# Last three steps of a two-convolution kernel written out on alternating PSUM banks, with a new way to finish and store the last half

## What is computed

```python
def reference(x, L0_conv_weight, L0_conv_threshold, L1_conv_kernel, L1_conv_bias):
    # x: (16, 32, 128, 128) float32
    # _gn: mean and variance over 16 groups of 2 channels, per image
    x = x + _L0_conv_ref(_gn(x), L0_conv_weight, L0_conv_threshold)   # 3x3, padding 1, weights masked by a score
    x = x + _L1_conv_ref(_gn(x), L1_conv_kernel, L1_conv_bias)        # 5x5 by FFT, same size, plus a bias per channel
    return x
```

## Time and profile before

| what | value |
|---|---|
| median of 3 runs | 835.81 us (834.25 to 837.2) |
| the profiled execution's own time | 834.83 us |
| its span, first to last instruction | 833.0 us |
| TensorE busy | 757.8 us (91%) |
| VectorE, ScalarE, GpSimd busy | 605.1, 336.1, 266.7 us |
| TensorE's granted clock, mean | 0.980 |
| DMA, mean over the span | 181 GB/s |

### The profile page before, as it was taken

The page is one execution under the profiler, slowest core; times in us unless marked ns, Lnnn a source line. Parts: engine busy times, 40 slices in busy tenths (PEclk is TensorE's granted clock), DMA queues, the critical chain, the costliest instruction groups (busy, mean ns, idle before and its releaser), DMA issues.

```text
span 833.0 us, 67770 instructions
## 1 busy us (share of the span) xinstructions
PE 757.8 (91%) x32302; PEld 541.3 (65%) x32302; DVE 605.1 (73%) x949; ACT 336.1 (40%) x289; POOL 266.7 (32%) x165
## 2 busy tenths in 40 slices
PE   0585579999999999999999999999999999998795
PEld 0342247787767677777778667867778777766463
DVE  6598368787878879787878788897978785745241
ACT  0352225444443536354444435363634444443410
POOL 1042022233333333232333333332323333333221
PEclk9998879999999999999999999999999999999998
DMA  8979986899897979898998979798987576753124
GB/s 178 209 154 224 218 183 152 192 219 213 194 218 164 221 190 223 195 222 194 219 209 201 213 171 231 177 223 192 221 195 177 138 177 153 155 132 90 43 50 101
DMA packets 234118, 150.59 MB, mean 181 GB/s; under 512 B 18592, under 2 KB 227552, under 8 KB 229984
## 3 DMA queue, kind: packets, MB, share of 16 engines
q1 hardware_dynamic: 228768, 144.67, 78.9%
q10 hardware_dynamic: 4608, 4.23, 2.1%
q0 software_dynamic: 704, 1.25, 0.7%
HBM read 75.60 MB, written 33.59 MB: 131 GB/s over the span
## 4 chain that ended last, share of the span: by engine, by line
PE 87%; issue 4%; DMA 3%; SPq 2%; ACT 1%; DVE 1%; ACTq 0%; POOLq 0%; DVEq 0%; POOL 0%
PE psum L772 66%; PE psum L790 21%; DMA x_bands<-x_dram 1%; DMA mid_bands<-mid 1%; SPq L259 1%; SPq L251 1%; ACT mid_bands L394 0%; DVE bn_in L559 0%; ACTq L455 0%; ACT conv_out L424 0%; ACT x_hi L387 0%; POOLq L57 0%; ACT x_hi L379 0%; SPq L240 0%; SPq L275 0%
## 5 line engine op out<-in xcount | busy, mean ns | idle before, releaser
L360 POOL TENSOR_TENSOR mid<-mid,conv_out 128x512 f32<-128x512 f32 x122 | 246.7, 2052 | 512.3 <-ACT conv_out L424 512.3
L772 PE MATMUL psum<-x_hi,s_hi 32*64 32x512 f16 x6656 | 200.9, 383 | 16.7 <-ACTq L455 6.6
L772 PE MATMUL psum<-x_hi,s_lo 32*64 32x512 f16 x6656 | 198.6, 378 | 1.6 <-issue 1.6
L772 PE MATMUL psum<-x_lo,s_hi 32*64 32x512 f16 x6656 | 198.3, 380 | 0.9 <-issue 0.5
L772 PEld LDWEIGHTS psum<-x_hi,s_hi 32*64 32x64 f16 x6656 | 126.6, 105 | 79.8 <-issue 12.1
L772 PEld LDWEIGHTS psum<-x_hi,s_lo 32*64 32x64 f16 x6656 | 141.7, 104 | 45.8 <-issue 4.6
L772 PEld LDWEIGHTS psum<-x_lo,s_hi 32*64 32x64 f16 x6656 | 105.7, 104 | 79.6 <-issue 10.6
L650 DVE SCALAR_TENSOR_TENSOR mid<-psum,unscale,x_own 128x1024 f32<-128x1024 f32 x64 | 79.2, 1279 | 97.1 <-PE psum L790 96.6
L424 ACT ACTIVATE conv_out<-psum,bias,unscale 128x512 f32<-128x512 f32 x122 | 85.2, 778 | 83.4 <-PE psum L772 83.4
L379 ACT ACTIVATE x_hi<-x_bands 128x2304 f16<-128x2304 f32 x32 | 67.8, 2119 | 119.8 <-PE psum L790 116.9
L387 ACT ACTIVATE x_hi<-mid_bands 128x2560 f16<-128x2560 f32 x32 | 74.8, 2339 | 69.9 <-PE psum L790 67.9
(11 more groups left out here) (77 smaller groups left out, 335.6 us busy)
## 6 DMA issues: line engine op xcount, KB each, us to landing
x_own<-x_dram SPq DMA_DIRECT2D x128, 256.0 KB, 5.0
mid_bands<-mid SPq DMA_DIRECT2D x372, 80.0 KB, 2.7
out_dram<-mid SPq DMA_DIRECT2D x116, 256.0 KB, 5.0
x_bands<-x_dram SPq DMA_DIRECT2D x96, 288.0 KB, 6.1
x_bands<-x_dram SPq DMA_DIRECT2D x32, 272.0 KB, 6.1
mid_bands<-mid SPq DMA_DIRECT2D x124, 64.0 KB, 2.7
every_mv<-mv_scratch ACTq DMA_DIRECT2D x16, 256.0 KB, 4.1
out_dram<-mid SPq DMA_DIRECT2D x24, 128.0 KB, 2.4
```

What stands on the lines that cost most here:

```text
L360: nc.gpsimd.tensor_tensor(m, m, conv_out[:, b, :], ALU.add).then_inc(out_added, 1)
L772: ins = nc.tensor.matmul(psum[2 * C * J:2 * C * (J + 1), bank + i, :].rearrange("p (a w) -> p a w", a=A), w[quad(i), at:at + 2, :].rearran ...
```

## The change

Four things are changed. TensorE's three last steps are written out one after another instead of looping; they use banks 0 to 3, 4 to 7, and 0 to 3 in turn (bank5), after one wait for bank3_go. ScalarE raises x5_hi_go for them before it takes the preceding half out of PSUM, and for the last two waits for VectorE's take of the half two before. GpSimd adds the bias to the last half's mid early, after its adds for half 29 (the mid of half 31 is complete then and has been moved on). The last half is finished by VectorE alone, in two operations that each read two banks of PSUM, scale them and add mid; each group of two banks is stored by two transfers from SP and two from ScalarE's queue.

```diff
+        LAST = HALVES - 1
+        LAST_GROUPS = (slice(HALF_BANKS, BANKS), slice(0, HALF_BANKS))
+        def bank5(k):
+            return X3_BANK if k >= LATE and (k - LATE) % 2 == 0 else X5_BANK
...
# SP, in place of the two store_out calls for the last half
+                    elif k == LAST:
+                        for g, banks in enumerate(LAST_GROUPS):
+                            sp.wait_ge(last_out, g + 1)
+                            store_out(k, banks, range(Q // 2))
...
# GpSimd
-            for k in range(HALVES):
+            for k in range(LAST):
                 for b in range(BANKS if k < LATE else HALF_BANKS):
                     add_out(k, b)
+                if k == LATE:
+                    pool.wait_ge(norm2, HALVES)
+                    m = mid[:, LAST % MID_SLOTS, :, :]
+                    nc.gpsimd.tensor_scalar(m, m, bias[:, 0:1], None, ALU.add).then_inc(bias_added, 1)
...
# ScalarE
-                nc.scalar.activation(conv_out[:, b, :], psum[:, X5_BANK + b, :], ACT.Identity,
+                nc.scalar.activation(conv_out[:, b, :], psum[:, bank5(k) + b, :], ACT.Identity,
...
-                if has5(s - 1):
+                if s > HALVES + 1:
+                    act.wait_ge(late_out, s - HALVES - 1)
+                if has5(s) and s >= HALVES:
+                    act.drain().then_inc(x5_hi_go, 1)
+                if has5(s - 1) and s <= LAST + LAG:
                     k = s - 1 - LAG
                     for b in range(BANKS if k < LATE else HALF_BANKS):
                         take_conv5(k, b)
-                if s > HALVES:
-                    act.wait_ge(late_out, s - HALVES)
-                if has5(s):
+                if has5(s) and s < HALVES:
                     act.drain().then_inc(x5_hi_go, 1)
...
+            for g, banks in enumerate(LAST_GROUPS):
+                act.wait_ge(last_out, g + 1)
+                for j in range(Q // 2, Q):
+                    act.dma_start(own_rows(out[LAST // 2], LAST % 2, j)[:, A * banks.start:A * banks.stop, :],
+                                  as_rows(mid, j, LAST % MID_SLOTS, banks)).then_inc(out_stored[LAST % MID_SLOTS], 16)
...
# VectorE (take_late also reads bank5(k) instead of X5_BANK)
-            take_late(HALVES - 1)
-            add_late(HALVES - 1)
+            dve.wait_ge(b5_whole, LAST + 1)
+            dve.wait_ge(bias_added, 1)
+            for at in LAST_GROUPS:
+                m = mid[:, LAST % MID_SLOTS, at, :]
+                nc.vector.scalar_tensor_tensor(m, psum[:, bank5(LAST) + at.start:bank5(LAST) + at.stop, :], unscale[:, 1:2], m,
+                                               ALU.mult, ALU.add).then_inc(last_out, 1)
...
# TensorE (pairs5_high, singles5 and pairs5_low take the bank; whole_step's reg_add stands before pairs5_low as before)
-                pe.br_lt(step, HALVES, on_true="whole_step", on_false="before_last").branch_hint(hint)
-            with nc.body("before_last", valid_engines=only):
-                pe.br("last_steps")
-            with nc.body("last_steps", valid_engines=only):
-                pairs5_high()
-                singles5()
-                pairs5_low(step)
-                pe.br_lt(step, STEPS, on_true="last_steps", on_false="all_done")
-            nc.switch_bb("all_done")
+                pe.br_lt(step, HALVES, on_true="whole_step", on_false="last_steps").branch_hint(hint)
+            nc.switch_bb("last_steps")
+            pe.wait_ge(bank3_go, 1)
+            for k in range(LATE, HALVES):
+                pairs5_high(bank5(k))
+                singles5(bank5(k))
+                pairs5_low(bank5(k))
```

More of the change, by code:

```diff
@@ L172, in two_blocks @@
         late_added = sem("late_added")
+        bias_added = sem("bias_added")
+        last_out = sem("last_out")
         def has3(s):
@@ L241, in load_own, with store_out @@
                                  ).then_inc(x_own_in[h % X_SLOTS], 16)
-            def store_out(k, banks):
-                for j in range(Q):
+            def store_out(k, banks, quads=range(Q)):
+                for j in quads:
                     sp.dma_start(own_rows(out[k // 2], k % 2, j)[:, A * banks.start:A * banks.stop, :],
@@ L667, in take_late @@
                 at = slice(HALF_BANKS, BANKS)
-                nc.vector.tensor_scalar(conv_out[:, at, :], psum[:, X5_BANK + at.start:X5_BANK + at.stop, :],
+                nc.vector.tensor_scalar(conv_out[:, at, :], psum[:, bank5(k) + at.start:bank5(k) + at.stop, :],
                                         unscale[:, 1:2], bias[:, 0:1], ALU.mult, ALU.add).then_inc(late_out, 1)
@@ L812, in singles3, with pairs5_high, singles5, pairs5_low @@
                 singles(s3_hi, x3_lo, K3, X3_BANK).then_inc(c3_whole, 1)
-            def pairs5_high():
+            def pairs5_high(bank=X5_BANK):
                 pe.wait_ge(x5_hi_go, 1)
-                pairs(s5_hi, x5_hi, K5, X5_BANK, start=True, every=x5_hi_go)
-                pairs(s5_lo, x5_hi, K5, X5_BANK)
-            def singles5():
+                pairs(s5_hi, x5_hi, K5, bank, start=True, every=x5_hi_go)
+                pairs(s5_lo, x5_hi, K5, bank)
+            def singles5(bank=X5_BANK):
                 pe.wait_ge(x5_lo_go, 1)
[L823 to L830, removed]
+                singles(s5_hi, x5_lo, K5, bank)
+                singles(s5_hi, x5_hi, K5, bank)
+                singles(s5_lo, x5_hi, K5, bank).then_inc(a5_whole, 1)
+            def pairs5_low(bank=X5_BANK):
+                pairs(s5_hi, x5_lo, K5, bank, every=x5_lo_go).then_inc(b5_whole, 1)
             def mix_mean(stat):
@@ L897, in _ @@
                 singles5()
-                pairs5_low(step)
-                pe.br_lt(step, HALVES, on_true="whole_step", on_false="before_last").branch_hint(hint)
-            with nc.body("before_last", valid_engines=only):
-                pe.br("last_steps")
-            with nc.body("last_steps", valid_engines=only):
-                pairs5_high()
-                singles5()
-                pairs5_low(step)
-                pe.br_lt(step, STEPS, on_true="last_steps", on_false="all_done")
-            nc.switch_bb("all_done")
+                pe.reg_add(step, step, 1)
+                pairs5_low()
+                pe.br_lt(step, HALVES, on_true="whole_step", on_false="last_steps").branch_hint(hint)
[5 more added lines that the diff above has]
+                pairs5_low(bank5(k))
 _INS = ["x", "L0_conv_weight", "L0_conv_threshold", "L1_conv_kernel", "L1_conv_bias"]
```

## The result

Twenty runs of each kernel gave 838.18 us for the changed one and 835.66 us for the one before: a ratio of 1.0031 with a 95% interval of 1.0021 to 1.0042, so +2.6 us. A second comparison (experiment 8) gave 836.39 against 835.88 us, 1.0007 (0.9993 to 1.0022). The change costs 0 to 3 us; +5.2 were forecast.

A forecast was written before the change was run, and what follows sets the result against it. TensorE, busy for 91% of the span, was taken as the bound, with block delivery of first-run code setting the late pace. Late steps +7.4 and tail -2.2 gave +5.2 us: 841.0 us on the median, range 834.5 to 847.

The forecast's parts named there:

- The mechanism: TensorE's late steps: first-run code arrives in blocks of 128 matmuls, one at a time, about 3.97 us apart; rerun code costs nothing.
- The 18 packets: Sign in the profile after: about 18 instruction packets on q8 after 758 us instead of 7.
- The first rival, blocks ahead of use: Late steps: straight-line fetching runs ahead and stalls vanish, 820.2 us, or 825.2 if the first block is waited for; chance 0.12.
- 11 more intervals of 3.97 us: Late steps from 783.71 us: 11 block deliveries, 43.7 us, putting the last matmul at 830.6 against 823.17, +7.4 us.
- up to 783.71 nothing differs: First late step: same timing as before up to 783.71 us, except the first stop, counted as 0 gain.
- The bound with 3.72: Late steps at the shortest interval seen: last matmul at 827.8 us, +4.7 us.
- the rival with 3.5: "Half of it": late intervals near 3.5 us as the DMA is mostly idle, 835.8 us, no change; chance 0.10.
- Worth 2 x 1.56, already spent: Alternating banks and earlier go-ahead remove two late-step stops of 1.56 us, already counted in the blocks' slower pace.
- The first stop: TensorE's wait after the loop, until 761.47 us: 0 gain, since it waits for the first block anyway; bound 0.5 us.
- Idle stretches of 1.5 us did not lower it: TensorE's clock: stayed at 1.00 after 1.5 us idle; the half clock from 762 to 765 us was left in.
- GpSimd's bias: Early bias for the last half: one 128x2048 operation of 5.9 us from about 792 us, cost 0.
- The tail: After the last matmul: forecast -2.2 us, between -1.8 (full DMA limits) and -3.6 (issue by one queue was part of the limit).

The follow-up runs named there:

- experiment 8: The changed kernel as it is, run again for a second trace, against the kernel before: 836.39 us, ratio 1.0007.
- Experiment 2: The kernel before with its three last steps written out and nothing else changed: 843.62 us, ratio 1.0093.
- experiment 4: The kernel before with singles3 ahead of pairs5_high and late steps jumping back to a label in whole_step, no code of their own: 839.5 us, ratio 1.0043.
- experiment 6: The kernel before with late steps on whole_step's resident code in the old order, a branch skipping singles3, and the new finish: 827.93 us, ratio 0.9904.
- experiment 1: The kernel before with the new finish of the last half alone (early bias, VectorE's two operations, stores by two queues): 833.77 us, ratio 0.9972.

## Why the prediction was wrong

**The mechanism was right.** That code run for the first time comes in blocks of 128 matmuls, one after another, was forecast from the earlier trace rows. The 18 packets and the stops in all three late steps came as written down. Experiment 2 shows the cost by writing out alone, experiments 4 and 6 show it vanish when the same matmuls run on resident code. The first rival, blocks ahead of use, fell.

**The step that failed is the size of one term**, "11 more intervals of 3.97 us" and, ahead of it, "up to 783.71 nothing differs". The late part grew by 3.6 and 2.4 us in the two traces and not by 7.4. There are two pieces:

- The interval. I took the mean of four, two of which, 4.28 and 4.13, were long. The eleven of the changed kernel average 3.77, ten of experiment 8 3.58 (783.12 to 818.96); without stores it is 3.65. From the start of the eleven, 784.75, to the last matmul are 44.6 us instead of the 46.9 forecast (830.6 - 783.71), 2.3 less. In experiment 8 it is 826.4 - 783.1 = 43.3, 3.6 less. Four intervals, two of them taken while a half was being stored, were too few for a term that multiplies the mean by 11. The bound with 3.72, +4.7 us, was nearer, and the rival with 3.5, +2.2 us on the late part and no change of the time, was nearer than the forecast to both traces. Part of that is luck: its interval was met by the second trace alone, and the shorter first late step, which it did not have, made up the rest.
- The first late step. From the end of the loop to the sixth block it took 25.1 us before and 23.6 in the changed kernel, though the first block came no sooner after the loop's end (764.74 - 761.1 = 3.6 against 761.96 - 758.57 = 3.4 us). The 5.88 us interval behind it was absent: the second block was there when the first was used up. Of the 1.5 us saved, 1.1 lie in the first three intervals (12.8 us against 13.9), 0.7 in the next two, and 0.3 are lost again ahead of them. Before, that fetch met the moves to mid_bands: its packet on q8 started 3.4 us after TensorE had begun the block ahead of it, with 212 GB/s on the DMA engines from 763 to 764.9, in the changed kernel 1.6 us after, with 120 GB/s from 764.8 to 767.7. That the moves are the reason is argued from this timing and was not tried. It does not hang on the banks alone: experiment 2 took 23.8 us too (783.33 - 759.58), experiment 1, which loops, 25.3.

The trace also shows what an interval is made of. For each of the eleven blocks of the changed kernel, the packet with the next block's code starts 1.1 to 1.9 us after TensorE has begun a block, and the next block is begun 2.3 to 2.7 us after that packet. For the block begun at 784.75 the packet came at 785.9, and the next block was begun at 788.47. So one block is fetched at a time, and only once TensorE has begun the block ahead of it. A block of pairs runs 3.46 us, nearly as long as that takes, and the stops behind it are 0.3 to 0.5 us; a block of singles runs 1.8 us, and where a block is mostly singles the stops are 1.7 to 2.3 us. Most of the added time lies there.

**The stops for the takes.** "Worth 2 x 1.56, already spent" in the pace of the blocks is right: experiment 2 against the changed kernel, 70.3 against 68.2 and 67.0, has 2.1 and 3.3 us back, around the 3.1. The first stop was forecast as 0 gain, and the block that arrives 3.7 us after TensorE has run out of code shows why.

**The clock.** "Idle stretches of 1.5 us did not lower it" held, but it was not the whole of it. Stops for code of 2.0 us lowered it in some traces and not in others. Stretches of experiment 8:

```profile
817.10:818.90 1.80, 0.00 (x0) 0.00 (x0) 0.00 (x0) 0.00 (x0) 0.00 (x0) 1.00 0.71 176
819.90:823.20 3.30, 3.30 (x80) 1.37 (x70) 0.00 (x0) 0.00 (x0) 0.00 (x0) 0.50 0.02 5
```

Behind a stop as long as at 820.53 in the changed kernel's first trace, which stayed at 1.00, 3.3 us ran at 1.2 GHz. This is in the 67.0 us, so the blocks alone cost less still.

**GpSimd's bias** was costed at nothing and 5.9 us long; it took 6.4 and nothing waited for it. **The tail** was forecast at -2.2 and is -2.0 in both traces and -2.3 in experiment 1. The last MB moved in 4.7 us, 831.4 to 836.1, where it took 4.6 with one issuing engine. DMA of the changed kernel, 830 to 837 us, in 40 slices of 0.175 us:

```profile
GB/s 0 0 0 0 0 0 0 0 38 202 184 120 149 255 296 263 269 313 313 304 249 211 252 293 275 275 284 249 281 293 284 208 85 41 9 0 0 0 0 0
```

The rule of the Trainium skill (DMA: Bandwidth & Descriptors, Issuing engines are not separate DMA queues), that issuing from several engines saves issue time alone, agrees with this. How the gain divides between VectorE's finish and the shorter issue no run shows.

**The sum.** With the sizes measured, +3.6 - 2.0 = +1.6 and +2.4 - 2.0 = +0.4 us, where +2.6 (1.8 to 3.5) and +0.6 us (-0.6 to 1.8) were timed. The rest in the first is at the size of the scatter of whole_step's first pass. That the change does not gain 10 us or more is settled. That it costs anything rests on the first comparison, since the interval of the second takes in 0; whether it is 0.6 or 2.6 us stays open.

## What to carry to other kernels

Count the instructions of a stretch before writing it out. Here 256 instructions of TensorE take 3.6 to 3.8 us to arrive in the mean and 1.8 to 3.5 us to run, so a loop body, or better a label in a body that has already run, beat straight code, most of all where the instructions are short. That was seen with a body of about 2030 instructions; no run here has a longer one. A skip of part of this body cost nothing that shows. When a term is an interval times a count, look for more samples of it under the same conditions than four; and weigh the parts of a change singly, since here one gained 2.3 us and another gave it all back.

## What the runs showed that was not expected

- The change of weight tile between 64 and 32 columns stops the weight loads, for 0.42 us one way and 0.23 the other, and one more change each way cost 0.33 us a step; moving 144 matmuls of `singles` by one place cost 8.4 us of 836.
- An idle stretch of 3.4 to 3.7 us in the weight loads was followed by 3.0 to 3.4 us of matmuls at 1.2 GHz, by 5.6 us in experiment 8; one of 2.1 us for the takes never was, and one of 2.3 us for code was in experiments 2 and 8 and was not in the first trace of the changed kernel.
- A body of about 2030 instructions ran 28 times with no packet on TensorE's instruction queue after the first pass, and its middle could be entered by a branch with no stop for code; the one packet behind it came 16 to 19 us after the loop's end.
